# Scan rounds of a selective scan: three of four rounds, in place of two of four, take their input products from ScalarE and TensorE's transposes

## The reference

```python
# x_s, z, B_s, C_s, dt from one projection; x_s after a causal convolution and silu
dt = softplus(einsum(dt, W_dt) + b_dt)
A = -exp(A_log)
def step(h, inp):                       # over the 256 tokens of a sequence
    dt_t, u_t, b_t, c_t = inp
    dA = exp(dt_t[..., None] * A)
    h = dA * h + dt_t[..., None] * b_t[:, None, :] * u_t[..., None]
    y = einsum('bdn,bn->bd', h, c_t)
    return (h, y)
y = (scan of step) + u * D
y = y * silu(z);  out = layernorm(residual + y @ W_out)
```

## Time and profile before

| | us |
|---|---|
| median of 3 runs | 782.1 (781.0 to 782.15) |
| profiled execution | 781.24 |
| span of its trace | 779.4 |
| PE busy | 658.2 (84%) |
| DVE busy | 622.9 (80%) |
| POOL busy | 429.1 (55%) |
| ACT busy | 417.2 (54%) |
| scan stage, first L977 to the end of the last L965 | 73.7 to 273.7 |

### The profile page before, as it was taken

The page is one execution under the profiler, slowest core; times in us unless marked ns, Lnnn a source line. Parts: engine busy times, 40 slices in busy tenths (PEclk is TensorE's granted clock), DMA queues, the critical chain, the costliest instruction groups (busy, mean ns, idle before and its releaser), DMA issues. The chain is left out here.

```text
span 779.4 us, 13077 instructions
## 1 busy us (share of the span) xinstructions
PE 658.2 (84%) x4791; PEld 430.8 (55%) x4800; DVE 622.9 (80%) x1519; ACT 417.2 (54%) x729; POOL 429.1 (55%) x380
## 2 busy tenths in 40 slices
PE   4997798898988833748899999999999999899994
PEld 1444444444444332634667667777666666667773
DVE  6479798999989686467688888888888888779886
ACT  1996786776767305444454444444444444355551
POOL 6113587696887848464665555555555555551222
PEclk9997799999999986789999999999999999999997
DMA  9003132332344100000000000000000000000001
GB/s 324 7 5 54 35 100 89 86 96 81 84 100 85 55 2 0 0 1 1 2 1 22 1 6 15 22 2 4 15 2 21 2 7 13 1 1 1 1 25 32
DMA packets 17297, 27.36 MB, mean 35 GB/s; under 512 B 2320, under 2 KB 7056, under 8 KB 16976
## 3 DMA queue, kind: packets, MB, share of 16 engines
q1 hardware_dynamic: 17232, 26.51, 12.8%
HBM read 25.32 MB, written 1.18 MB: 34 GB/s over the span
## 5 line engine op out<-in xcount | busy, mean ns | idle before, releaser
L573 POOL TENSOR_TENSOR arena<-arena 128x1024 f32<-128x1024 f32 x64 | 150.0, 2359 | 52.3 <-PE psum L1322 27.3
L991 DVE TENSOR_TENSOR_SCAN arena<-arena,psum 128x1024 f32<-128x1024 f32 x64 | 141.8, 2267 | 3.3 <-issue 2.0
L1322 PE MATMUL psum<-arena,Cs 128*128 128x512 f32 x256 | 121.9, 599 | 1.2 <-POOL arena L573 1.2
L510 POOL TENSOR_TENSOR ve<-mv,eps 128x4 f32<-128x4 f32 x52 | 16.0, 307 | 191.7 <-DVE mv L889 191.7
L705 ACT ACTIVATE arena<-arena 128x510 f32<-128x510 f32 x128 | 84.8, 711 | 51.8 <-DVE arena L991 49.8
L620 POOL TENSOR_TENSOR arena<-arena,mhalf 128x32 f32<-128x32 f32 x16 | 86.8, 5428 | 2.3 <-DVE arena L1108 2.3
L1214 PE MATMUL psum<-Cs,arena 128*128 128x128 f32 x240 | 39.6, 290 | 42.9 <-ACT arena L748 25.9
L1407 PE MATMUL psum<-arena,Wl 128*128 128x512 f32 x128 | 67.4, 639 | 8.6 <-DVE arena L1092 5.3
L1322 PEld LDWEIGHTS psum<-arena,Cs 128*128 128x128 f32 x256 | 45.2, 191 | 46.3 <-issue 35.0
L1214 PEld LDWEIGHTS psum<-Cs,arena 128*128 128x128 f32 x240 | 28.6, 147 | 62.6 <-issue 28.3
L1305 PE MATMUL psum<-Cs,arena 128*128 128x128 f32 x256 | 35.2, 284 | 23.9 <-ACT arena L727 20.7
(11 more groups left out here) (172 smaller groups left out, 1415.6 us busy)
## 6 DMA issues: line engine op xcount, KB each, us to landing
arena<-c_rows_by_state SPq DMA_DIRECT2D x32, 512.0 KB, 4.8
Wl<-wl SPq DMA_DIRECT2D x4, 384.0 KB, 3.2
Wd<-wd SPq DMA_DIRECT2D x1, 1100.0 KB, 10.8
X<-x SPq DMA_DIRECT2D x4, 256.0 KB, 6.4
Sel<-sel SPq DMA_DIRECT2D x1, 1024.0 KB, 8.3
Wl<-wl SPq DMA_DIRECT2D x4, 256.0 KB, 3.0
out<-X SPq DMA_DIRECT2D x4, 256.0 KB, 2.3
Cs<-const SPq DMA_DIRECT2D x1, 614.0 KB, 9.2
```

Of the source, the lines that this page charges most:

```text
L573: pool.tensor_tensor(Hc[:, h], Hs[:, r, h], Crows[:, r], ALU.mult).then_inc(hc_ready, 1)
L991: dve.tensor_tensor_scan(Hs[:, turn % 2, h], Da[:, h], rows_of(turn, h), 0.0, ALU.mult, ALU.add).then_inc(scanned, 1)
L1322: ins = pe.matmul(bank[h], ident, Hc[:, h, group(e)], start=False, stop=False, skip_group_check=True)
```

## The change

The list of turned rounds is made longer. Before, every odd round is turned (16 of 32); after it all rounds but those divisible by four (24 of 32). Everything else follows from the list. The eight rounds 2, 6, 10, 14, 18, 22, 26 and 30 pass from rows to turned.

```diff
-TURNED = [t for t in range(ROUNDS) if t % 2 == 1]
+TURNED = [t for t in range(ROUNDS) if t % 4 != 0]
```

## The result

The kernel after the change takes 794.83 us (median of 4 runs, 794.35 to 796.0) against 781.97 before: ratio 1.0159, interval 1.0125 to 1.0193. It is 12.9 us slower; 795 was forecast. The profiled execution took 796.0 us, span 794.2. The last L965 ends at 287.70 us, where it ended at 273.67: 14.0 of the 14.8 us between the two profiled executions are in the scan stage, and what lies behind it takes 506.5 us in place of 505.8. The stage itself is 13.7 us longer (213.7 in place of 200.0); it also began 0.3 us later.

The account below looks back on a forecast made before the run. DVE was taken as the bound, PE close behind; after the change, waits among ACT, PE and POOL lengthen the scan stage. 781.24 + 6.5 (walk) + 6.8 (clock) = 794.5 us, so median 795; range 785 to 800.

Parts of the forecast that it names:

- What it takes away and adds: Eight newly turned rounds: DVE drops 17.9 us of products; ACT gains 25.6 us of pieces, PE 14.4 of transposes less 7.0.
- The walk: Scan stage laid out in program order with waits: a group takes 49.18 us against 47.80, together +6.5 us.
- (1): One decay buffer per half: ACT can't work ahead, its half-round with pieces takes 2.84 us against a scan's 2.18.
- (2): PE's adds queue behind its wait for ACT's pieces, holding up POOL's product and DVE's scan two rounds on.
- (3): Three turned rounds in a row: PE's half-round is 2.62 us, above 2.18, and the 0.86 us skip matmul falls there.
- The clock: PE's 3.56 us waits ahead of rounds 10, 18, 26 lower its clock: 5.1 us, plus 1.7 in the opening, 6.8.
- since the wait is longer than both that led to a fall: PE's 3.56 us wait exceeds the 3.39 and 2.93 us waits elsewhere with low clock, so 6.8 us was taken.
- The walk's rival, no falls at all: PE's clock level holds through the 3.56 us waits: 788.6 us, range 785.5 to 790, chance 0.31.
- The sum: Whole kernel: profiled execution 781.24 + 6.5 + 6.8 = 794.5 us, its median 0.9 higher, so 795 predicted.
- DVE as the bound: Scan stage: ACT's pieces still hide, DVE's 17.9 us come off, 764 us; chance 0.06.
- the late C rows: C rows' DMA lands in 8 us or more, not 4.8, stopping POOL in each turned run: 803 us, chance 0.08.
- a low level through a whole turned run: Transposes count for nothing, so PE runs whole turned runs at half speed: up to 15.7 us a group, 851, chance 0.03.

Follow-up runs that it names:

- e1: Kernel after the change with twelve bf16 matmuls ahead of PE's wait for the pieces of rounds 10, 18 and 26: 789.67 us, ratio 1.0104.
- e3: Kernel after the change with a second decay buffer for each half, the expert weights' load moved behind the scan stage: 773.23 us, ratio 0.9897.
- e2: Kernel after the change with PE's adds of states put ahead of the buffer fills: 778.28 us, ratio 0.9962.
- e7: Kernel before the change with PE's adds of states put ahead of the buffer fills: 777.98 us, ratio 0.9943.
- e5: Kernel after the change with both alterations, adds ahead of the fills on PE and two decay buffers: 767.45 us, ratio 0.9832.
- e10: Half the change against the kernel before: only rounds 2, 10, 18 and 26 turned in addition: 792.84 us, ratio 1.016.
- e9: Half the change against the kernel before: only rounds 6, 14, 22 and 30 turned in addition: 787.04 us, ratio 1.0081.
- e4: Kernel after the change with only the first of four token tiles of each piece computed on ACT: 775.32 us, ratio 0.9924.
- e11: Kernel after the change with twelve bf16 matmuls ahead of PE's wait for the pieces of rounds 2, 10, 18 and 26: 788.0 us, ratio 1.010.
- e6: Kernel before the change with adds ahead of the fills on PE and two decay buffers: 775.31 us, ratio 0.9926.
- e8: Kernel after, adds ahead of fills, two decay buffers, plus twelve bf16 matmuls ahead of PE's wait for round 1's pieces: 766.06 us, ratio 0.9814.

## Why the prediction was right

**What it takes away and adds**: confirmed. L977 x16, L727 x192 with nearly the same durations (median 1.226 us for 1.216, and 0.493 for 0.492); ACT's half-round with pieces is 2.82 us between scans.

**The walk**: 49.18 us a group at full clock; 49.27 in e1, where the clock is full. Its small waits ahead of scans, forecast at 0.4 to 1.6 us, are 0.24 to 1.44 us in the trace where the level is full, and up to 2.22 behind a fall; the gate's wait in a group is 1.15, the last one's 6.3 as forecast. Its three reasons: (1) shown by e3; (2) shown by e2 and e7, and in e3 it goes with (1); (3) seen only where the other two are gone, in e5, and not tested by an edit of its own.

**The clock**: forecast three falls at 1.7 us and one longer low stretch in the opening at 1.7, 6.8 us. Measured: 1.75 us a fall, three times, which is the group of 51.02 for 49.27. In the opening the stage takes 58.87 us to the gate of group 0, 55.52 before: 3.4 more, where the walk's 1.5 and the clock's 1.7 are 3.2. The level came up 17.32 us after the start of the stage, before the change 14.18; the 3.1 us between them cost 1.6 by an estimate from the half found with e1 and e10. The last group is 4.0 us longer, 2.3 + 1.7. The wait of PE was 3.44 us for 3.56.

What the prediction had wrong here is the rule by which it expected the falls, "since the wait is longer than both that led to a fall". The length of the wait does not decide: e10 has the same wait once without a fall, and falls stand behind waits of 2.45 us (e9), as long as those in the kernel before that brought none, and of 2.16 to 2.24 us (e1, e4, e11). That there were just three falls in this execution, as forecast, is in part luck. Its figure of 3.4 us for a low stretch held inside the steady groups; behind the stage the trace of the kernel before has longer ones as well (309.8 to 316.6 us). The walk's rival, no falls at all, was not reached with this order of the work: e1 comes nearest, at 789.67 with one.

**The sum**: 13.3 forecast on the profiled execution, 14.8 measured there (14.0 at the last gate, 0.7 behind it), 12.9 between the medians. The median was put 0.9 us above the profiled execution and came out 1.2 below it, so that 794.83 came so near to 795 is in part luck. The 2 us allowed for the part behind the stage were a little too few: over the kernels of the table it takes 504.1 to 508.3 us in place of 505.8, and its code is the same in all (but for the load of the expert weights in e3, e5, e6 and e8).

**Rivals**: DVE as the bound is out, the late C rows too (POOL waited 1.2 us for them in all), and a low level through a whole turned run is out: all low stretches inside the steady groups lasted 3.4 us. By the Trainium skill, "TensorE: Matmul & The Clock Gate", section "Part 4: PE-mode transpose", the full clock does not engage for transposes, which do not count as busy in the way that matmuls do. The traces show three turned rounds in a row, 48 transposes among adds, at 1.00 throughout in e5; where only transposes follow a wait, no run isolates them.

## What to carry to other kernels

Sums of work by engine tell what a change could gain; whether it does is told by the depth of the buffers between the engines, laid out for one period in program order with the waits. An instruction that waits in an in-order queue holds up all behind it: put the one whose result others wait for ahead of it. A change that fails may be good once an obstacle is gone: look for the obstacle before giving up the change. And what takes the obstacle away belongs in the kernel before as well, or its own gain is put down to the change, as with e2 without e7.

## What the runs showed of the hardware

The granted clock of TensorE does not follow from the length of an idle wait alone. These are all waits of PE over 1.9 us in the steady groups of the thirteen kernels, and whether the level fell between 0.1 us ahead of their end and 1.3 us behind it:

| wait, us | where | level fell | level stayed |
|---|---|---|---|
| 3.43 to 3.44 | after (3), e10 (3) | 5 | 1 (e10, 138.47) |
| 2.45 to 2.46 | before (3), e9 (3) | 1 (e9, 141.66) | 5 |
| 2.16 to 2.24 | after (1), e1 (1), e4 (3), e11 (1) | 4 (e1, e11, two in e4) | 2 |

These ten are all the falls in those groups; the waits of 1.2 to 1.6 us brought none. Two of the waits of 2.2 us, from the timeline of PE in e4, the first without a fall and the second with one:

```profile
129.43 1.06 PE L1305 MATMUL psum<-Cs,arena 128*128 128x128 f32 x8 [2.24 <-ACT arena L727]
...
175.54 1.94 PE L1305 MATMUL psum<-Cs,arena 128*128 128x128 f32 x8 [2.24 <-ACT arena L727]
```

The waits of 2.2 us brought a fall more often than those of 2.45. In the steady groups every low stretch lasted 3.4 us, at exactly half speed. It cost about its half when PE was the link that all waited for: 1.75 us from e1 to after, 1.69 and 1.62 between two groups of e10 and of e4, 1.45 in e9. Twelve bf16 matmuls inside the wait (2.76 us) prevented it all six times, in e1 and e11, but in both kernels the level fell later, behind the wait of 2.2 us in the last group.
